# Two attention layers on one core: where the prologue's maxima are kept, and the order of a head's loads

## The chip, the cores and the metric

The kernel runs on one core of a Trainium2 chip. The metric is the device time of one execution in microseconds (us), as the median of several runs. A core has five engines that work side by side and wait for each other by semaphores: TensorE (PE, the matmuls; PEld is its weight load), VectorE (DVE), ScalarE (ACT), GpSimd (POOL) and SyncE (SP), which here only issues transfers (DMA).

## The reference

A two-layer transformer on 2048 tokens of width 128. The change touches only the attention of both layers, which has 16 heads of width 64:

```python
# layer 0
scores = jnp.einsum('bhsd,bhtd->bhst', q, k) * scale
attn = jax.nn.softmax(scores, axis=-1)
out = jnp.einsum('bhst,bhtd->bhsd', attn, v)
# layer 1: q and k are rotated, and a bias by distance is added
dist = jnp.abs(pos[None, :] - pos[:, None])
kb = -p * jnp.log1p(a * dist)
attn = jax.nn.softmax(scores + kb[None], axis=-1)
out = jnp.einsum('bhqk,bhkd->bhqd', attn, v)
```

Around it stand layer norms, a gated feed-forward part in each layer (in layer 1 eight experts with a router), and the projections.

## The kernel before, in words

The program is a row of stages, each a block that starts when all engines have finished the one before. `attention_stage` is called twice, with `bias=False` and `bias=True`; its names begin with `a0_` and `a1_`, and the profile leaves the number out.

The stage before has written q and k to the chip's memory, each split in two float16 tensors, high and low halves (`qk_high`, `qk_low`). The stage works by head (16) and, in a head, by chunks of 512 queries (4): 64 chunks `n`. A chunk has eight steps `s` of 256 keys.

**Loads.** SyncE loads a head `h` by eight transfers of 256 KB: twice `qh`, `kh`, `ql`, `kl`, for the lower and the upper 64 partitions (L595 to L598), and in layer 1 the bias table `tab` of 1984 KB as a ninth (L600). All count on one semaphore, `loaded`. There is room for two heads. Head 1 is issued when head 0 has landed, head `h` from 2 on when the scores of head `h - 2` have been read.

**Maxima.** The softmax takes each query's maximum off first. `maxima(n, j)`, `j` from 0 to 7, is a pair of matmuls of the high halves alone (L612, L613), 128 queries by 1024 keys into the PSUM buffer `jb`. VectorE reduces them to one maximum per query, in layer 0 by `reduce_max` (L774), in layer 1 by an operation that adds the bias from `tab` and takes the maximum in one (L769); that one writes its sums to `junk`, which nobody reads, and the maximum by a second small instruction, the accumulator read. There is one `jb`, so each pair waits for the reduction before it (L608). When the eight are done, `merge(n)` on VectorE (L780), `divide_maxima(n)` on ScalarE (L721), `row(n)` on TensorE (L621) and `row(n)` on ScalarE (L726) make of them the rows that are subtracted.

**Scores.** `scores(n, s)` is eight matmuls into one of two halves of `st` (L639): high by high, high by low, low by high, and the maxima. In layer 0 ScalarE exponentiates out of `st` (L740). In layer 1 VectorE adds the bias out of `st` into an SBUF ring (L794, `add_bias`), and ScalarE exponentiates there (L733). `values` multiplies by v (L650), GpSimd sums the exponentials (L847), `project` and VectorE's L798 and L804 make the output.

**Order.** It is written out by hand for each engine. Maxima run two chunks ahead of the scores (`AHEAD = 2`). So there is a prologue, in which only maxima run: chunk 0's eight, `row(0)`, chunk 1's eight. Then in the main loop each step of chunk `n` also issues `maxima(n + 2, s)`. In layer 0 the first of these stands ahead of the first scores; in layer 1 `scores(0, 0)` and `scores(0, 1)` stand ahead of it.

Of the kernel before, what the change touches and what calls it, by code (L numbers as in the profile page):

```python
# [6 lines left out]
BF16 = mybir.dt.bfloat16  # L7
ALU = mybir.AluOpType
ACT = mybir.ActivationFunctionType
AX = mybir.AxisListType  # L10

P = 128
# [3 lines left out]
DH = 64  # L16
NT = S // P
QC = 512
NC = S // QC
# [15 lines left out]
AHEAD = 2  # L35
NJ = 8
# [509 lines left out]
def attention_stage(nc, k, layer, bias=False):  # L546

    with ExitStack() as ctx:
        m = Memory(nc, ctx)
        g = f"a{layer}_"  # L550
        qh, ql = m.sb(g + "qh", [P, 2 * S], F16), m.sb(g + "ql", [P, 2 * S], F16)
        kh, kl = m.sb(g + "kh", [P, 2 * S], F16), m.sb(g + "kl", [P, 2 * S], F16)
# [8 lines left out]
        st = m.ps(g + "st", [P, 2, 2 * QC])  # L561
# [2 lines left out]
        xb = m.ps(g + "xb", [P, QC])  # L564
        if bias:
            tab = m.sb(g + "tab", [P, 2, BW])
            junk = m.sb(g + "junk", [P, 2 * QC], BF16)
        ones_set, loaded = m.sem(g + "ones_set"), m.sem(g + "loaded")
        max_ready, max_done = m.sem(g + "max_ready"), m.sem(g + "max_done")
        merged, m4_done = m.sem(g + "merged"), m.sem(g + "m4_done")  # L570
        row_ready, row_done = m.sem(g + "row_ready"), m.sem(g + "row_done")
# [2 lines left out]
        pv_done, ov_saved = m.sem(g + "pv_done"), m.sem(g + "ov_saved")  # L574
        proj_ready, proj_done, rs_done = m.sem(g + "proj_ready"), m.sem(g + "proj_done"), m.sem(g + "rs_done")
        st_read = added if bias else exp_done
        loads = 8 + (1 if bias else 0)
        pool_adds = NS - 1
        block = ctx.enter_context(nc.Block())

        def summed_by(step):
            n, s = divmod(step, NS)
# [2 lines left out]
        @block.sync  # L585
        def _(sp):
            for h in range(H):
                if h >= 1:
                    sp.wait_ge(loaded, 16 * loads * h)
                if h >= 2:  # L590
                    sp.wait_ge(st_read, NS * NC * (h - 1))
                at = slice((h % 2) * S, (h % 2 + 1) * S)
                pr, half = h // 2, slice((h % 2) * DH, (h % 2 + 1) * DH)
                for low in (slice(0, DH), slice(DH, P)):
                    sp.dma_start(qh[low, at], k.qk_high[0, pr][half, :]).then_inc(loaded, 16)  # L595
                    sp.dma_start(kh[low, at], k.qk_high[1, pr][half, :]).then_inc(loaded, 16)
                    sp.dma_start(ql[low, at], k.qk_low[0, pr][half, :]).then_inc(loaded, 16)
                    sp.dma_start(kl[low, at], k.qk_low[1, pr][half, :]).then_inc(loaded, 16)  # L598
                if bias:
                    sp.dma_start(tab[:, h % 2, :], k.bias_rows(h)).then_inc(loaded, 16)  # L600

        @block.tensor
        def _(pe):
            def maxima(n, j):
                if j == 0 and n % NC == 0:
                    pe.wait_ge(loaded, 16 * loads * (n // NC + 1))
                if NJ * n + j >= 1:
                    pe.wait_ge(max_done, NJ * n + j)  # L608
                base = (n // NC % 2) * S
                q0 = base + (n % NC) * QC + (j // 2) * P  # L610
                k0 = base + (j % 2) * 2 * QC
                nc.tensor.matmul(jb[:, 0:QC], qh[0:DH, q0:q0 + P], kh[0:DH, k0:k0 + QC], start=True, stop=True)  # L612
                nc.tensor.matmul(jb[:, QC:2 * QC], qh[DH:P, q0:q0 + P], kh[DH:P, k0 + QC:k0 + 2 * QC],  # L613
                                 start=True, stop=True).then_inc(max_ready, 1)

            def row(n):
# [8 lines left out]
            def scores(n, s):  # L625
                step = NS * n + s
                base = (n // NC % 2) * S
                q0 = base + (n % NC) * QC
                if s == 0:
                    pe.wait_ge(row_done, n + 1)  # L630
                if step >= 2:
                    pe.wait_ge(st_read, step - 1)
                for r, (keys, queries) in enumerate(((kh, qh), (kh, ql), (kl, qh), (lower, rows))):
                    for t in range(2):
                        half = slice(t * DH, (t + 1) * DH)
                        k0 = base + (2 * s + t) * P
                        w = lower[half, :] if r == 3 else keys[half, k0:k0 + P]
                        x = rows[half, n % 2, :] if r == 3 else queries[half, q0:q0 + QC]
                        last = nc.tensor.matmul(st[:, step % 2, t * QC:(t + 1) * QC], w, x,  # L639
                                                start=(r == 0), stop=(r == 3))  # L640
                last.then_inc(st_ready, 1)
# [122 lines left out]
        def _(ve):  # L764
            def maxima(n, j):
                ve.wait_ge(max_ready, NJ * n + j + 1)
                if bias:
                    c0 = 2 * QC + (n % NC) * QC + (j // 2) * P - (j % 2) * 2 * QC
                    nc.vector.tensor_tensor_reduce(  # L769
                        out=junk[:, :], in0=jb[:, :], in1=tab[:, n // NC % 2, c0:c0 + 2 * QC][:, ::-1], scale=1.0,  # L770
                        scalar=-3.0e38, op0=ALU.add, op1=ALU.max, accum_out=mx[:, j // 2, j % 2:j % 2 + 1])\
                      .then_inc(max_done, 1)
                else:
                    nc.vector.reduce_max(mx[:, j // 2, j % 2:j % 2 + 1], jb[:, :], AX.X).then_inc(max_done, 1)  # L774

            def merge(n):
                ve.wait_ge(max_done, NJ * n + NJ)
# [395 lines left out]
```

## Time and profile before

| | us |
|---|---|
| three runs, median | 3418.86 |
| their lowest and highest | 3417.58, 3419.49 |
| the profiled execution, time | 3421.26 |
| its span in the trace | 3419.4 |
| attention, layer 0: first load issued to start of the loop | 193.0 to 237.8 |
| attention, layer 1: first load issued to start of the loop | 2050.6 to 2098.7 |
| layer 1's loop ends about | 3409 |

Over the span TensorE is busy 92%, GpSimd 70%, VectorE 69%, ScalarE 42%. Times in the rows count from the start of the span. A line number is that of the kernel before. A busy TensorE is not TensorE at its peak. PEclk is the clock that it was granted, as a share of 2.4 GHz; 0.50 is 1.2 GHz.

### The profile page before, as it was taken

What the parts mean: (1) busy time and instruction counts of PE and PEld (TensorE: products, weight loads), DVE (VectorE), ACT (ScalarE), POOL (GpSimd) and SP (SyncE); (2) the same over time, 40 slices, a digit from 0 to 9 for tenths busy, and PEclk for the clock granted to TensorE, in tenths of its full rate; (3) what the DMA queues carried; (4) which work ended last, traced back from release to release, by engine and by line L of the source; (5) the groups of instructions that cost most, each with busy time, mean ns of one, the idle gap of its engine ahead of it and who ended that gap; (6) DMA issues with size and microseconds to landing.
All of it is one profiled execution on the core that took longest, in us unless ns stands there. A gap on an engine that the chain in (4) does not pass through costs nothing. (4 is left out here: it accounts for less than half of the span.)

```text
span 3419.4 us, 47107 instructions
## 1 busy us (share of the span) xinstructions
PE 3133.3 (92%) x18389; PEld 1247.1 (36%) x18389; DVE 2356.3 (69%) x3610; ACT 1427.8 (42%) x1609; POOL 2394.8 (70%) x1080
## 2 busy tenths in 40 slices
PE   5949999999999999948888985999999999999997
PEld 3414444444444444333333431333333333333333
DVE  6545555555555555351211696999999999999996
ACT  3325555555555555510000222555554555545544
POOL 0019999999999999900000383888888888888887
PEclk9969999999999999958888997999999999999998
DMA  3341111112111111010000133111111111112200
GB/s 80 126 123 26 25 26 26 26 26 49 26 26 26 26 26 25 1 51 0 0 0 0 49 148 97 49 49 49 49 49 49 49 49 49 49 54 60 60 23 13
DMA packets 53617, 148.69 MB, mean 43 GB/s; under 512 B 17155, under 2 KB 24076, under 8 KB 51220
## 3 DMA queue, kind: packets, MB, share of 16 engines
q1 hardware_dynamic: 53396, 145.67, 15.5%
q8 instruction: 147, 2.41, 0.3%
q14 instruction: 74, 0.61, 0.1%
HBM read 110.78 MB, written 34.87 MB: 43 GB/s over the span
## 5 line engine op out<-in xcount | busy, mean ns | idle before, releaser
L847 POOL TENSOR_TENSOR a_total<-a_total,room 128x1024 f32<-128x1024 f32 x768 | 1815.3, 2364 | 141.9 <-ACT room L740 37.3
L650 PE MATMUL a_ov<-room,va 128*64 128x512 f32 x4096 | 991.6, 605 | 0.0
L774 DVE TENSOR_REDUCE a_mx<-a_jb 128x1 f32<-128x1024 f32 x512 | 627.2, 1225 | 508.6 <-PE a_jb L613 508.6
L733 ACT ACTIVATE room<-room,sscale 128x1024 f32<-128x1024 f32 x512 | 588.4, 1149 | 650.5 <-DVE room L794 650.4
L740 ACT ACTIVATE room<-a_st,sscale 128x1024 f32<-128x1024 f32 x512 | 548.8, 1111 | 556.6 <-PE a_st L639 556.6
L769 DVE CUSTOM_DVE_ANT_0 a_junk<-a_jb,a_tab 128x1024 bf16<-128x1024 f32 x512 | 623.8, 1218 | 50.9 <-PE a_jb L613 34.6
L794 DVE TENSOR_TENSOR room<-a_st,a_tab 128x1024 f32<-128x1024 f32 x512 | 623.7, 1219 | 5.2 <-PE a_st L639 3.0
L612 PE MATMUL a_jb<-a_kh,a_qh 64*128 64x512 f16 x1024 | 396.6, 387 | 102.0 <-DMA a_tab<-bias_line 30.9
L847 POOL TENSOR_TENSOR a_total<-room 128x1024 f32<-128x1024 f32 x128 | 302.5, 2363 | 182.4 <-ACT room L733 135.6
L639 PE MATMUL a_st<-a_qh,a_kh 64*128 64x512 f16 x2048 | 394.9, 382 | 21.0 <-DVE room L794 21.0
L650 PEld LDWEIGHTS a_ov<-room,va 128*64 128x64 f32 x4096 | 248.4, 136 | 423.6 <-issue 363.7
L613 PE MATMUL a_jb<-a_kh,a_qh 64*128 64x512 f16 x1024 | 396.7, 387 | 0.0
L639 PE MATMUL a_st<-a_qh,a_kl 64*128 64x512 f16 x2048 | 389.5, 377 | 0.0
L639 PE MATMUL a_st<-a_ql,a_kh 64*128 64x512 f16 x2048 | 389.5, 377 | 0.0
L639 PE MATMUL a_st<-a_rows,a_lower 64*128 64x512 f16 x2048 | 389.4, 377 | 0.0
L496 POOL COPY wo<-wo 128x2048 f32<-128x2048 f32 x1 | 1.9, 1891 | 409.9 <-POOLq L986 409.9
L612 PEld LDWEIGHTS a_jb<-a_kh,a_qh 64*128 64x128 f16 x1024 | 95.9, 94 | 457.8 <-issue 153.1
L639 PEld LDWEIGHTS a_st<-a_qh,a_kh 64*128 64x128 f16 x2048 | 99.4, 94 | 317.8 <-issue 155.5
L667 PEld LDWEIGHTS a_xb<-ones,a_total 128*128 128x128 f32 x1024 | 135.0, 192 | 124.1 <-issue 124.1
L671 PE MATMUL a_xb<-wo,a_osb 128*128 128x128 f32 x1024 | 178.9, 298 | 0.0
L849 POOL TENSOR_TENSOR a_total<-a_total 128x512 f32<-128x512 f32 x128 | 163.0, 1273 | 10.0
L667 PE MATMUL a_xb<-ones,a_total 128*128 128x1 f32 x1024 | 156.6, 257 | 14.5 <-issue 12.5
(181 smaller groups left out, 2616.1 us busy)
## 6 DMA issues: line engine op xcount, KB each, us to landing
a_tab<-bias_line SPq DMA_DIRECT2D x16, 1984.0 KB, 12.1
qk_high<-q_oh SPq DMA_DIRECT2D x32, 512.0 KB, 2.6
qk_low<-q_ol SPq DMA_DIRECT2D x32, 512.0 KB, 3.6
a_qh<-qk_high SPq DMA_DIRECT2D x64, 256.0 KB, 4.9
a_kh<-qk_high SPq DMA_DIRECT2D x64, 256.0 KB, 5.7
a_ql<-qk_low SPq DMA_DIRECT2D x64, 256.0 KB, 6.3
a_kl<-qk_low SPq DMA_DIRECT2D x64, 256.0 KB, 6.7
ex_w<-in_L_ffn_W SPq DMA_DIRECT2D x1, 2048.0 KB, 10.5
```

Source lines behind the costliest of these rows:

```text
L612: nc.tensor.matmul(jb[:, 0:QC], qh[0:DH, q0:q0 + P], kh[0:DH, k0:k0 + QC], start=True, stop=True)
L613: nc.tensor.matmul(jb[:, QC:2 * QC], qh[DH:P, q0:q0 + P], kh[DH:P, k0 + QC:k0 + 2 * QC], start=True, stop=True).then_inc(max_ready, 1)
L639: last = nc.tensor.matmul(st[:, step % 2, t * QC:(t + 1) * QC], w, x, start=(r == 0), stop=(r == 3))
L650: last = nc.tensor.matmul(ov[t * DH:(t + 1) * DH, :], k.va[:, 2 * s + t, h * DH:(h + 1) * DH], prob[:, step % RING, t * QC:(t + 1) * QC], ...
L667: nc.tensor.matmul(xb[:, 2 * P + t:2 * P + t + 1], total[:, n % 2, q:q + P], k.ones[:, 0:1], start=(t == 0), stop=True, skip_group_check=True)
L671: last = nc.tensor.matmul(xb[:, t * P:(t + 1) * P], osb[:, q:q + P], k.wo[:, n // NC, :], start=False, stop=True, skip_group_check=True)
L733: nc.scalar.activation(prob[:, r, :], prob[:, r, :], ACT.Exp, scale=k.sscale[:, layer:layer + 1])\
L740: nc.scalar.activation(prob[:, r, :], st[:, step % 2, :], ACT.Exp, scale=k.sscale[:, layer:layer + 1])\
L769: nc.vector.tensor_tensor_reduce(out=junk[:, :], in0=jb[:, :], in1=tab[:, n // NC % 2, c0:c0 + 2 * QC][:, ::-1], scale=1.0, scalar=-3.0e38 ...
L774: nc.vector.reduce_max(mx[:, j // 2, j % 2:j % 2 + 1], jb[:, :], AX.X).then_inc(max_done, 1)
L794: nc.vector.tensor_tensor(p[:, :, ::-1], x[:, :, ::-1], window, ALU.add).then_inc(added, 1)
L847: nc.gpsimd.tensor_tensor(t, first, prob[:, step % RING, :], ALU.add).then_inc(summed, 1)
```

## The change

- **Buffers of the maxima.** In the prologue (the first 16 maxima, `FIRST = AHEAD * NJ`) the function `scratch` gives `st[0]`, `st[1]` and `jb` in turn; from the seventeenth on `jb` alone, as before. TensorE's wait in the prologue is for the maximum three before.
- **Scores.** The first two scores wait for all 16 maxima, since `st` was in use.
- **`junk`** has two buffers; a maximum of layer 1 also waits for the one two before it.
- **Loads.** A head's four transfers of high halves come first, then the table, then the four of low halves, which count on a semaphore of their own, `low_loaded`. For head 0 SyncE waits until the first group has landed before it issues the low halves. TensorE's first maximum of a head waits for `loaded`, its first score for `low_loaded` too.

```diff
-            junk = m.sb(g + "junk", [P, 2 * QC], BF16)
-        ones_set, loaded = m.sem(g + "ones_set"), m.sem(g + "loaded")
+            junk = m.sb(g + "junk", [P, 2, 2 * QC], BF16)
+        ones_set, loaded, low_loaded = m.sem(g + "ones_set"), m.sem(g + "loaded"), m.sem(g + "low_loaded")
...
-        loads = 8 + (1 if bias else 0)
+        loads = 4 + (1 if bias else 0)
+        FIRST = AHEAD * NJ
...
+        def scratch(n, j):
+            i = NJ * n + j
+            return jb[:, :] if i >= FIRST or i % 3 == 2 else st[:, i % 3, :]
...
                     sp.wait_ge(loaded, 16 * loads * h)
+                    sp.wait_ge(low_loaded, 16 * 4 * h)
...
-                    sp.dma_start(ql[low, at], k.qk_low[0, pr][half, :]).then_inc(loaded, 16)
-                    sp.dma_start(kl[low, at], k.qk_low[1, pr][half, :]).then_inc(loaded, 16)
                 if bias:
                     sp.dma_start(tab[:, h % 2, :], k.bias_rows(h)).then_inc(loaded, 16)
+                if h == 0:
+                    sp.wait_ge(loaded, 16 * loads)
+                for low in (slice(0, DH), slice(DH, P)):
+                    sp.dma_start(ql[low, at], k.qk_low[0, pr][half, :]).then_inc(low_loaded, 16)
+                    sp.dma_start(kl[low, at], k.qk_low[1, pr][half, :]).then_inc(low_loaded, 16)
...
-                if NJ * n + j >= 1:
+                if NJ * n + j >= FIRST:
                     pe.wait_ge(max_done, NJ * n + j)
+                elif NJ * n + j >= 3:
+                    pe.wait_ge(max_done, NJ * n + j - 2)
+                o = scratch(n, j)
...
+                if n % NC == 0 and s == 0:
+                    pe.wait_ge(low_loaded, 16 * 4 * (n // NC + 1))
                 if step >= 2:
                     pe.wait_ge(st_read, step - 1)
+                else:
+                    pe.wait_ge(max_done, FIRST)
...
                 if bias:
+                    i = NJ * n + j
+                    if i >= 2:
+                        ve.wait_ge(max_done, i - 1)
```

How the instructions stand on the engines. SyncE at the start of layer 1's attention, before:

```order
L595 DMA a1_qh<-qk_high 64x2048
L596 DMA a1_kh<-qk_high 64x2048
L597 DMA a1_ql<-qk_low 64x2048
L598 DMA a1_kl<-qk_low 64x2048
L595 DMA a1_qh<-qk_high 64x2048
L596 DMA a1_kh<-qk_high 64x2048
L597 DMA a1_ql<-qk_low 64x2048
L598 DMA a1_kl<-qk_low 64x2048
L600 DMA a1_tab<-bias_line 128x3968
L595 DMA a1_qh<-qk_high 64x2048 [waits a1_loaded]
```

and now, in the same place:

```order
L601 DMA a1_qh<-qk_high 64x2048
L602 DMA a1_kh<-qk_high 64x2048
L601 DMA a1_qh<-qk_high 64x2048
L602 DMA a1_kh<-qk_high 64x2048
L604 DMA a1_tab<-bias_line 128x3968
L608 DMA a1_ql<-qk_low 64x2048 [waits a1_loaded]
L609 DMA a1_kl<-qk_low 64x2048
L608 DMA a1_ql<-qk_low 64x2048
L609 DMA a1_kl<-qk_low 64x2048
L601 DMA a1_qh<-qk_high 64x2048 [waits a1_low_loaded,a1_loaded]
```

The table has moved from the ninth place to the fifth, and the low halves stand behind a wait. TensorE at the start of layer 0's prologue, before:

```order
L612 MATMUL a0_jb<-a0_kh,a0_qh 128x512 [waits a0_loaded,a0_ones_set]
L613 MATMUL a0_jb<-a0_kh,a0_qh 128x512
L612 MATMUL a0_jb<-a0_kh,a0_qh 128x512 [waits a0_max_done]
L613 MATMUL a0_jb<-a0_kh,a0_qh 128x512
L612 MATMUL a0_jb<-a0_kh,a0_qh 128x512 [waits a0_max_done]
```

and now:

```order
L624 MATMUL a0_st<-a0_kh,a0_qh 128x512 [waits a0_loaded,a0_ones_set]
L625 MATMUL a0_st<-a0_kh,a0_qh 128x512
L624 MATMUL a0_st<-a0_kh,a0_qh 128x512
L625 MATMUL a0_st<-a0_kh,a0_qh 128x512
L624 MATMUL a0_jb<-a0_kh,a0_qh 128x512
L625 MATMUL a0_jb<-a0_kh,a0_qh 128x512
L624 MATMUL a0_st<-a0_kh,a0_qh 128x512 [waits a0_max_done]
```

The first wait for a maximum stands at the fourth pair, not at the second. TensorE at the end of layer 1's prologue, the last pair and the first scores, before:

```order
L612 MATMUL a1_jb<-a1_kh,a1_qh 128x512 [waits a1_max_done]
L613 MATMUL a1_jb<-a1_kh,a1_qh 128x512
L639 MATMUL a1_st<-a1_qh,a1_kh 128x512 [waits a1_row_done]
L639 MATMUL a1_st<-a1_qh,a1_kh 128x512
L639 MATMUL a1_st<-a1_ql,a1_kh 128x512 x2
```

and now:

```order
L624 MATMUL a1_st<-a1_kh,a1_qh 128x512 [waits a1_max_done]
L625 MATMUL a1_st<-a1_kh,a1_qh 128x512
L655 MATMUL a1_st<-a1_qh,a1_kh 128x512 [waits a1_max_done,a1_low_loaded,a1_row_done]
L655 MATMUL a1_st<-a1_qh,a1_kh 128x512
L655 MATMUL a1_st<-a1_ql,a1_kh 128x512 x2
```

The order is the same; the first score waits for three things instead of one.

## Rows read from the trace of the kernel before

**Rows 1.** Stretches: bounds, length, busy us (instructions) of PE, PEld, DVE, ACT, POOL; PEclk, DMA, GB/s

```profile
205.30:237.40 32.10, 10.30 (x36) 2.05 (x36) 19.76 (x17) 2.12 (x3) 0.00 (x0) 0.50 0.30 66
237.40:241.70 4.30, 4.26 (x20) 1.36 (x20) 1.39 (x2) 1.31 (x2) 0.00 (x0) 0.50 0.00 0
243.10:300.00 56.90, 56.81 (x398) 21.97 (x400) 33.70 (x41) 29.57 (x34) 53.59 (x25) 1.00 0.01 1
...
2112.00:3350.00 1238.00, 1209.18 (x8030) 446.20 (x8027) 1215.58 (x1883) 627.16 (x671) 1088.68 (x488) 1.00 0.17 48
```

**Rows 2.** Timeline, loads of layer 0: start, us, engine, line, what [idle before, releaser]

```profile
194.83 0.60 SPq L598 DMA_DIRECT2D a_kl<-qk_low  x1
...
197.38 0.60 SPq L598 DMA_DIRECT2D a_kl<-qk_low  x1
...
205.31 0.58 PE L612 MATMUL a_jb<-a_kh,a_qh 64*128 64x512 f16 x1 [21.48 <-DMA a_kl<-qk_low]
```

**Rows 3.** One line, L598 (kl) of layer 0's head 0: issue to landing

```profile
DMA to landing us min/median/max: 5.5/6.6/7.8
```

**Rows 4.** Timeline, loads of layer 1

```profile
2054.89 0.60 SPq L598 DMA_DIRECT2D a_kl<-qk_low  x1
2055.53 0.58 SPq L600 DMA_DIRECT2D a_tab<-bias_line  x1
...
2067.86 0.58 PE L612 MATMUL a_jb<-a_kh,a_qh 64*128 64x512 f16 x1 [30.90 <-DMA a_tab<-bias_line]
```

**Rows 5.** One line, L598 (kl) of layer 1's head 0: issue to landing

```profile
DMA to landing us min/median/max: 5.8/7.0/8.3
```

**Rows 6.** Timeline, layer 0's prologue, VectorE and TensorE

```profile
206.03 1.23 DVE L774 TENSOR_REDUCE a_mx<-a_jb 128x1 f32<-128x1024 f32 x1 [18.17 <-PE a_jb L613]
...
207.96 1.23 DVE L774 TENSOR_REDUCE a_mx<-a_jb 128x1 f32<-128x1024 f32 x1 [0.71 <-PE a_jb L613]
...
237.44 0.60 PE L612 MATMUL a_jb<-a_kh,a_qh 64*128 64x512 f16 x1 [1.32 <-DVE a_mx L774]
```

**Rows 7.** Timeline, layer 1's prologue and its end, VectorE and TensorE

```profile
2069.78 0.08 DVE L769 DVE_READ_ACCUMULATOR2_ANT a_mx<- 128x1 f32 x1
2069.92 0.10 PEld L612 LDWEIGHTS a_jb<-a_kh,a_qh 64*128 64x128 f16 x1 [1.95 <-DVE a_mx L769]
...
2070.57 1.23 DVE L769 CUSTOM_DVE_ANT_0 a_junk<-a_jb,a_tab 128x1024 bf16<-128x1024 f32 x1 [0.71 <-PE a_jb L613]
...
2072.51 1.23 DVE L769 CUSTOM_DVE_ANT_0 a_junk<-a_jb,a_tab 128x1024 bf16<-128x1024 f32 x1 [0.71 <-PE a_jb L613]
...
2084.57 0.61 PE L613 MATMUL a_jb<-a_kh,a_qh 64*128 64x512 f16 x1
...
2085.32 1.22 DVE L769 CUSTOM_DVE_ANT_0 a_junk<-a_jb,a_tab 128x1024 bf16<-128x1024 f32 x1 [1.69 <-PE a_jb L613]
...
2098.65 0.64 PE L639 MATMUL a_st<-a_qh,a_kh 64*128 64x512 f16 x2
...
2100.05 0.08 DVE L769 DVE_READ_ACCUMULATOR2_ANT a_mx<- 128x1 f32 x1
...
2100.68 1.22 DVE L794 TENSOR_TENSOR room<-a_st,a_tab 128x1024 f32<-128x1024 f32 x1 [0.35 <-PE a_st L639]
```

**Rows 8.** Timeline, VectorE in layer 1's loop

```profile
2416.52 1.22 DVE L769 CUSTOM_DVE_ANT_0 a_junk<-a_jb,a_tab 128x1024 bf16<-128x1024 f32 x1
...
2417.66 1.22 DVE L794 TENSOR_TENSOR room<-a_st,a_tab 128x1024 f32<-128x1024 f32 x1
```

**Rows 9.** Timeline, VectorE: an operation, and reductions of which each waits for the last

```profile
72.88 1.23 DVE L287 TENSOR_SCALAR rope<-rope 128x2048 f32<-128x2048 f32 x1
74.02 1.21 DVE L335 TENSOR_REDUCE tf_hi<-va 128x1 f32<-128x1024 f32 x1
75.27 1.22 DVE L336 TENSOR_REDUCE tf_lo<-va 128x1 f32<-128x1024 f32 x1
```

**Rows 10.** One line, L788, around 2415: the semaphore instruction ahead of a bias add

```profile
L788 DVEq EVENT_SEMAPHORE  x1: 50/50/50, 2415.8 to 2415.8; - x1
```

More of the change, by code:

```diff
@@ L611, in maxima @@
                 k0 = base + (j % 2) * 2 * QC
-                nc.tensor.matmul(jb[:, 0:QC], qh[0:DH, q0:q0 + P], kh[0:DH, k0:k0 + QC], start=True, stop=True)
-                nc.tensor.matmul(jb[:, QC:2 * QC], qh[DH:P, q0:q0 + P], kh[DH:P, k0 + QC:k0 + 2 * QC],
+                nc.tensor.matmul(o[:, 0:QC], qh[0:DH, q0:q0 + P], kh[0:DH, k0:k0 + QC], start=True, stop=True)
+                nc.tensor.matmul(o[:, QC:2 * QC], qh[DH:P, q0:q0 + P], kh[DH:P, k0 + QC:k0 + 2 * QC],
                                  start=True, stop=True).then_inc(max_ready, 1)
@@ L767, in maxima @@
                 if bias:
+                    i = NJ * n + j
+                    if i >= 2:
+                        ve.wait_ge(max_done, i - 1)
                     c0 = 2 * QC + (n % NC) * QC + (j // 2) * P - (j % 2) * 2 * QC
                     nc.vector.tensor_tensor_reduce(
-                        out=junk[:, :], in0=jb[:, :], in1=tab[:, n // NC % 2, c0:c0 + 2 * QC][:, ::-1], scale=1.0,
+                        out=junk[:, i % 2, :], in0=scratch(n, j), in1=tab[:, n // NC % 2, c0:c0 + 2 * QC][:, ::-1], scale=1.0,
                         scalar=-3.0e38, op0=ALU.add, op1=ALU.max, accum_out=mx[:, j // 2, j % 2:j % 2 + 1])\
@@ L773, in maxima @@
                 else:
-                    nc.vector.reduce_max(mx[:, j // 2, j % 2:j % 2 + 1], jb[:, :], AX.X).then_inc(max_done, 1)
+                    nc.vector.reduce_max(mx[:, j // 2, j % 2:j % 2 + 1], scratch(n, j), AX.X).then_inc(max_done, 1)
             def merge(n):
```

## The prediction

> **What bounds the kernel now.** Attention runs twice, in layer 0 without a bias and in layer 1 with one. I read the stretches first, for the engine that is busy in each, then the timeline of both prologues. In the main loops TensorE is busy 56.81 of 56.90 us in layer 0, and VectorE 1215.58 of 1238.00 us in layer 1 [rows 1]. So VectorE's idle time in layer 0's loop costs nothing, and what matters there is TensorE; in layer 1 it is VectorE. Before each loop stands a stretch that neither bounds: in layer 0's prologue TensorE is busy 10.30 of 32.10 us and VectorE 19.76 [rows 1], and ahead of that both wait for the loads.
>
> The loads: in layer 0 the first matmul starts at 205.31, released by the last of eight transfers of 256 KB, issued at 197.38 [rows 2]. In layer 1 the bias table is the ninth, issued at 2055.53, and the first matmul starts at 2067.86, released by it [rows 4].
>
> The maxima: TensorE fills the single buffer `jb`, VectorE reduces it, TensorE waits for that. Layer 0's reductions start at 206.03 and 207.96: 1.93 us apart, of which 1.23 is work and 0.71 waiting for the next pair of matmuls [rows 6]. Layer 1's start at 2070.57 and 2072.51, 1.94 us apart [rows 7]. Sixteen stand in each prologue.
>
> **Part 1, the loads.** The first four transfers of head 0 are now the high halves. The last of them takes the place in SyncE's queue that the first `kl` transfer has today: issued at 194.83, landed 5.5 us later, at 200.3. The last of the eight is issued at 197.38 and lands 7.8 us later, at 205.2 [rows 2, 3]. Between the two lie four landings of 1.2 us: they come in the order of issue at a constant rate. The first matmul moves from 205.3 to 200.4, **4.9 us** off layer 0. In layer 1 the eighth lands at 2054.89 + 8.3 = 2063.2; the fourth, issued 2.55 us before it as in layer 0, at 2052.3 + 5.8 = 2058.1 [rows 4, 5]. The table has landed by 2067.8, 4.6 us behind what stands ahead of it. Put behind the fourth it lands at 2062.7, **5.1 us** earlier. Bounds for both: 4.5 and 5.5 us.
>
> The low halves are issued once the rest has landed, in layer 0 from 200.4 to some 203; by today's 5.5 to 7.8 us they are there by 211. The first score that reads them comes at about 221.6, by the sum below. Ten microseconds cover them, and as many in layer 1. Behind SyncE's new wait are queued head 0's low halves and then head 1's loads, which TensorE needs two chunks into the loop, so they are covered too. Without that cover each microsecond of lateness would be one of the path.
>
> **Part 2, the rotation.** With `st[0]`, `st[1]` and `jb` TensorE may be two pairs ahead of the reduction in progress. From the start of a pair to the start of its reduction pass 0.65 us (2069.92 to 2070.57) [rows 7], less than two reductions take, so VectorE runs back to back. At what distance, no row shows for two maxima in a row. Two kinds of rows bound it. In layer 1's loop a bias add starts 1.14 us behind a maximum, whose accumulator read lies in between, and does not wait for it [rows 8]. Two reductions of which the second waits for the first start 1.25 us apart [rows 9]. The new maxima don't wait for the one before, so I take 1.15 us and keep 1.26 as the other end. A chunk of eight maxima has seven such steps. Layer 0: 2 x 7 x (1.93 - 1.15) = **10.9 us**. Layer 1: 2 x 7 x (1.94 - 1.15) = **11.1 us**. With 1.26 it would be 9.4 and 9.5. The way from a chunk's merge over ScalarE and TensorE's row to the next maximum stays, since `row(0)` still stands between the chunks.
>
> **Part 3, what now waits.** The first two scores write into `st`, so they wait for all sixteen maxima. In layer 0 a pair for chunk 2 that needs all sixteen stands ahead of them already (237.44) [rows 6]: nothing is added. In layer 1 the scores stand ahead of it. Today they start at 2098.65, while the last maximum is still to run, and the first bias add follows at 2100.68, only 0.63 us behind the last accumulator read at 2100.05 [rows 7]. In the change that read is followed by the handover to TensorE (2069.78 to 2069.92, 0.14 us) and by the scores' own 2.03 us (2098.65 to 2100.68): 2.17 us instead of 0.63, a **loss of 1.5 us**. Queued behind the waiting scores are TensorE's next maxima and values, and VectorE and ScalarE wait for the scores, so the loss is on the path. Bounds 1.2 and 1.9.
>
> **Part 4, the second `junk` buffer.** It adds a wait for `max_done` to nearly all 512 maxima of layer 1, on the engine that bounds its loop; here a small cost would weigh. What is waited for is the maximum before the last, long done. An operation with several waits gets a semaphore instruction of its own. The bias add has one today, of 50 ns; for the add that starts at 2417.66 it stands at 2415.8, nearly two operations early, and the add still starts 1.14 us behind its forerunner [rows 8, 10]. I cost it at nothing. The cover is that VectorE's queue is read ahead. Where it is not, it costs: the first maximum of chunk 1 has such an instruction that waits for its matmuls, and starts 0.75 us behind the pair (2084.57 to 2085.32), not 0.65 [rows 7].
>
> **Sum.** Layer 0: 4.9 + 10.9 = 15.8. Layer 1: 5.1 + 11.1 - 1.5 = 14.7. Together 30.5 us. The profiled run took 3421.26 us (its span of 3419.4 and 1.9 around it); 30.5 off makes 3390.8. The median of the runs, 3418.86, is 2.4 lower, so the forecast is **3388.4 us**. The bounds of the loads and of the handover make it 3387 to 3391.
>
> **The rivals.**
> *The maxima don't overlap.* They come 1.26 us apart. For it: the reductions 1.25 us apart. Against it: each of those waits for the one before, and the first of them, which does not, starts 1.14 us behind its forerunner (72.88 to 74.02) [rows 9]. It gives back 0.11 x 28 = 3.1 us: 3391.5. The Trainium skill has a rule to this effect (VectorE: DVE Perf Modes, The DRAIN you can't avoid): the next operation does not start until the pipe is empty. By that rule the time would be this rival's; this trace disagrees for the loop's operations, which take 1.22 us and start 1.14 us apart [rows 8].
>
> *TensorE's clock rises in the prologue.* Today it is granted 0.50 (1.2 GHz) through layer 0's prologue and for 4.3 us of dense work behind it, then 1.00 [rows 1]. The change packs the same 10.3 us of matmuls into some 21 us. If that raises it, the dense stretch runs at 2.4 GHz: half of 4.3 us in layer 0, as much at the start of layer 1 less what VectorE's own pace keeps, and some tenths for shorter ways from pair to reduction. Together 4 us less: 3384.4. If it rises later than today, because the prologue starts at another moment, up to 2 us more: 3390.4. The Trainium skill (TensorE: Matmul & The Clock Gate, What's actually happening) says that the throttled clock is the default and activity releases it. By that rule this rival is open; the row shows only that a third of the time busy did not do it.
>
> *The new waits cost VectorE (this one ends slower).* Place: each maximum of layer 1's loop. Price: the 0.10 us of a semaphore instruction that is not taken early, x 512 = 51 us, on an engine busy 98% of that stretch: 3388.4 + 51 = 3439. The gain is gone from 30.5 / 512 = 0.06 us each. Against it stands the bias add, which carries the same burden for nothing.
>
> *The loads don't come earlier*, because transfers in flight share the engines evenly: the 10 us go, 3398. Against it stand the landings 1.2 us apart.
>
> **How the numbers follow.** The forecast 0.60, maxima without overlap 0.12, the clock early 0.16, the loads 0.05, the waits 0.03, and 0.04 for a change that has no effect at all. The range from 3383.0 to 3394.0 takes in the first three with the bounds of the costs and leaves out 0.12. A measurement of this kernel tells about 0.2%, 7 us, from no change, and only the last two cases lie there or above: faster 0.94, same 0.03, slower 0.03.
>
> **What would show it.** The first matmul 5.6 us behind the issue of the fourth transfer in layer 0, today 10.5. The maxima of both prologues 1.15 us apart. In layer 1 the first bias add 2.2 us behind the last accumulator read. From there to the end of the stage each loop as long as now. It would be wrong if a loop got longer, if the granted clock were 1.00 ahead of the first score, or if a low half released a matmul.

## The result, and the profile after

The kernel before took 3418.25 us (median of four runs, 3417.58 to 3419.49), the changed one 3389.22 us (four runs, 3386.0 to 3390.83). The ratio is 0.9913, with an interval from 0.9896 to 0.9931: 29.0 us less. The profiled execution of the changed kernel is the 3386.0 us one, its span is 3384.2 us.

The stretches of the changed kernel that answer to [rows 1]: bounds, length, busy us (instructions) of PE, PEld, DVE, ACT, POOL, then PEclk, DMA share, GB/s. They are layer 0's prologue, the dense work behind it, a piece of its loop, and nearly all of layer 1's loop.

```profile
197.40:218.30 20.90, 9.55 (x36) 2.01 (x36) 18.44 (x17) 2.12 (x3) 0.00 (x0) 0.50 0.67 151
218.40:222.00 3.60, 3.60 (x20) 1.32 (x20) 1.31 (x2) 1.12 (x2) 0.00 (x0) 0.58 0.00 0
228.00:284.90 56.90, 56.90 (x400) 22.43 (x396) 33.95 (x43) 28.98 (x33) 53.94 (x26) 1.00 0.00 1
2080.00:3315.00 1235.00, 1206.15 (x8007) 445.23 (x8004) 1212.81 (x1880) 625.33 (x670) 1085.57 (x487) 1.00 0.17 48
```

The prologue is 20.9 us long instead of 32.1, and VectorE is busy in 18.4 of them. The two loops look as they did: TensorE busy throughout in layer 0, VectorE 98% busy in layer 1. The loads of layer 0 in the timeline (start, us, engine, line, what), with the row for L602 (`kh`) of head 0, answer to [rows 2, 3]:

```profile
192.24 0.60 SPq L602 DMA_DIRECT2D a_kh<-qk_high  x1
197.33 0.45 SPq L608 DMA_DIRECT2D a_ql<-qk_low  x1
...
197.45 0.58 PE L624 MATMUL a_st<-a_kh,a_qh 64*128 64x512 f16 x1 [16.32 <-DMA a_kh<-qk_high]
```

```profile
DMA to landing us min/median/max: 4.1/4.6/5.1
```

The fourth transfer lands 5.1 us behind its issue and releases the first matmul. In layer 1 the table releases it, issued fifth, as [rows 4, 5] had it ninth:

```profile
2032.63 0.58 SPq L604 DMA_DIRECT2D a_tab<-bias_line  x1
2041.87 0.44 SPq L608 DMA_DIRECT2D a_ql<-qk_low  x1
...
2041.99 0.58 PE L624 MATMUL a_st<-a_kh,a_qh 64*128 64x512 f16 x1 [25.35 <-DMA a_tab<-bias_line]
```

VectorE in layer 0's prologue, and the first pair of the loop on TensorE, for [rows 6] ("x2" and 2.35 are two reductions in one row):

```profile
201.57 2.35 DVE L793 TENSOR_REDUCE a_mx<-a_st 128x1 f32<-128x1024 f32 x2
203.83 1.21 DVE L793 TENSOR_REDUCE a_mx<-a_jb 128x1 f32<-128x1024 f32 x1
204.97 2.34 DVE L793 TENSOR_REDUCE a_mx<-a_st 128x1 f32<-128x1024 f32 x2
...
218.34 0.60 PE L624 MATMUL a_jb<-a_kh,a_qh 64*128 64x512 f16 x1 [2.78 <-DVE a_mx L793]
```

Three maxima take 204.97 - 201.57 = 3.40 us: 1.13 us apart, none waits for its pair. The end of layer 1's prologue, VectorE and TensorE, for [rows 7]:

```profile
2060.74 1.22 DVE L788 CUSTOM_DVE_ANT_0 a_junk<-a_jb,a_tab 128x1024 bf16<-128x1024 f32 x1
2061.88 0.08 DVE L788 DVE_READ_ACCUMULATOR2_ANT a_mx<- 128x1 f32 x1
2061.88 1.22 DVE L788 CUSTOM_DVE_ANT_0 a_junk<-a_st,a_tab 128x1024 bf16<-128x1024 f32 x1
2063.03 0.08 DVE L788 DVE_READ_ACCUMULATOR2_ANT a_mx<- 128x1 f32 x1
...
2065.25 1.22 DVE L813 TENSOR_TENSOR room<-a_st,a_tab 128x1024 f32<-128x1024 f32 x1 [1.95 <-PE a_st L655]
```

```profile
2063.26 0.61 PE L655 MATMUL a_st<-a_qh,a_kh 64*128 64x512 f16 x2 [2.92 <-DMA a_kl<-qk_low]
```

The maxima stand 1.14 us apart. The first bias add comes 2065.25 - 2063.03 = 2.22 us behind the last accumulator read, not 0.63: the scores start 0.23 us behind that read, and then VectorE waits for them. The profile names a low half as the releaser of the first score. It is a wait for three things, and which of them ended it is settled below.

VectorE in layer 1's loop, for [rows 8], and the semaphore instruction that now stands ahead of a maximum, for [rows 10]:

```profile
2384.86 1.22 DVE L813 TENSOR_TENSOR room<-a_st,a_tab 128x1024 f32<-128x1024 f32 x1
2386.00 1.22 DVE L788 CUSTOM_DVE_ANT_0 a_junk<-a_jb,a_tab 128x1024 bf16<-128x1024 f32 x1
```

```profile
L786 DVEq EVENT_SEMAPHORE  x510: 21/21/1734, 2044.0 to 3321.5; - x170
```

There are 510 of them, of 21 ns in the median, and a maximum still starts 1.14 us behind the bias add.

Where the time went, read from the timelines of both kernels in the same way: "load" from the first load's issue to the first matmul; "chunks" from there to the second chunk's merge; "handover" in layer 0 from that merge to the first exponential, in layer 1 from the last accumulator read to the first bias add; "loop" from there to the first operation of the block behind attention; "stage" the whole. (In layer 1 "chunks" and "handover" overlap by the 0.12 us between the last read and the merge.) All in us; the experiments of the next section stand in the same table.

| | L0 load | chunks | handover | loop | stage | L1 load | chunks | handover | loop | stage | both |
|---|---|---|---|---|---|---|---|---|---|---|---|
| before | 12.29 | 32.11 | 2.38 | 1225.02 | 1271.80 | 17.30 | 32.31 | 0.63 | 1309.02 | 1359.14 | 2630.9 |
| changed | 7.01 | 20.87 | 2.38 | 1224.41 | 1254.67 | 11.77 | 21.15 | 2.22 | 1309.34 | 1344.37 | 2599.0 |
| a2 (changed, again) | 7.40 | 20.88 | 2.38 | 1224.30 | 1254.96 | 11.83 | 21.15 | 2.23 | 1309.36 | 1344.45 | 2599.4 |
| e1 loads only | 7.33 | 32.11 | 2.38 | 1224.24 | 1266.06 | 12.04 | 32.30 | 0.63 | 1309.32 | 1354.17 | 2620.2 |
| e2 rotation only | 12.47 | 20.87 | 2.38 | 1225.05 | 1260.77 | 17.04 | 21.16 | 2.22 | 1308.80 | 1349.10 | 2609.9 |
| e3 two buffers | 7.40 | 20.88 | 1.25 | 1224.66 | 1254.19 | 11.97 | 21.16 | 0.31 | 1308.95 | 1342.27 | 2596.5 |
| e4 wait in prologue | 7.21 | 20.87 | 2.38 | 1225.04 | 1255.50 | 11.95 | 21.15 | 2.23 | 1309.32 | 1344.54 | 2600.0 |
| e5 filler | 7.36 | 22.20 | 2.20 | 1224.74 | 1256.50 | 13.12 | 22.05 | 1.38 | 1308.44 | 1344.87 | 2601.4 |
| e6 two buffers, filler | 7.17 | 22.00 | 0.19 | 1224.63 | 1253.99 | 11.99 | 22.36 | 0.32 | 1308.45 | 1343.00 | 2597.0 |
| e7 wait for the last | 7.21 | 23.62 | 2.38 | 1226.22 | 1259.43 | 11.98 | 24.41 | 2.23 | 1309.30 | 1347.80 | 2607.2 |
| e8 two, light filler | 7.04 | 20.87 | 1.25 | 1225.00 | 1254.16 | 11.98 | 21.15 | 0.70 | 1309.01 | 1342.73 | 2596.9 |
| e9 two, slice of qh | 5.91 | 20.87 | 1.25 | 1224.04 | 1252.07 | 10.45 | 21.15 | 0.31 | 1309.74 | 1341.54 | 2593.6 |
| e10 e8 and e9 | 5.70 | 20.87 | 1.26 | 1224.13 | 1251.96 | 10.48 | 21.16 | 0.71 | 1309.64 | 1341.87 | 2593.8 |

Attention gives 17.1 us in layer 0 and 14.8 in layer 1, 31.9 together. The span gives 35.2. The other 3.3 us lie in blocks that the change does not touch: 2.6 ahead of layer 0's first load (it is issued at 190.44, before at 193.02; over all these traces between 190.4 and 193.5), 0.6 between the two stages (582.6 to 586.8 over all) and 0.1 at the end. So two executions of the same code differ by some 3 us there, and the stages are compared by this table rather than by the spans.

### The profile page after: what moved, and what is told of

Same layout as the page of the kernel before. It is cut to its first block and busy times, and to the rows that moved or that the text cites. A ratio compares the mean times of both kernels' runs of the same rounds, so it can differ in the third digit from the quotient of the medians.

```text
span 3384.2 us, 47620 instructions
## 1 busy us (share of the span) xinstructions
PE 3129.0 (92%) x18389; PEld 1247.0 (37%) x18389; DVE 2353.5 (70%) x3610; ACT 1427.8 (42%) x1609; POOL 2395.2 (71%) x1080
## 5 line engine op out<-in xcount | busy, mean ns | idle before, releaser
L793 DVE TENSOR_REDUCE a_mx<-a_jb 128x1 f32<-128x1024 f32 x501 | 613.4, 1224 | 480.2 <-PE a_jb L625 480.2
L788 DVE CUSTOM_DVE_ANT_0 a_junk<-a_jb,a_tab 128x1024 bf16<-128x1024 f32 x501 | 610.1, 1218 | 18.8 <-PE a_jb L625 2.5
L624 PE MATMUL a_jb<-a_kh,a_qh 64*128 64x512 f16 x1002 | 383.4, 383 | 16.4 <-DVE a_mx L793 5.7
L625 PE MATMUL a_jb<-a_kh,a_qh 64*128 64x512 f16 x1002 | 383.5, 383 | 0.0
```

The costliest lines, as they stand in the source:

```text
L624: nc.tensor.matmul(o[:, 0:QC], qh[0:DH, q0:q0 + P], kh[0:DH, k0:k0 + QC], start=True, stop=True)
L625: nc.tensor.matmul(o[:, QC:2 * QC], qh[DH:P, q0:q0 + P], kh[DH:P, k0 + QC:k0 + 2 * QC], start=True, stop=True).then_inc(max_ready, 1)
L788: nc.vector.tensor_tensor_reduce(out=junk[:, i % 2, :], in0=scratch(n, j), in1=tab[:, n // NC % 2, c0:c0 + 2 * QC][:, ::-1], scale=1.0, sc ...
L793: nc.vector.reduce_max(mx[:, j // 2, j % 2:j % 2 + 1], scratch(n, j), AX.X).then_inc(max_done, 1)
```

## The experiments

The theory was that of the prediction: loads 10 us, rotation 22 us, minus 1.5 us at layer 1's first scores. All diffs are against the changed kernel unless they say otherwise. The kernel before, run beside them, took 3422.2 us in the first group (e1 to e4), 3420.26 in the second (a2 and e5 to e7) and 3419.69 in the third (e8 to e10); ratios are to those. "..." in a diff stands for lines left out.

**One part at a time (e1, e2), and the changed kernel again (a2).** e1 keeps the new order of the loads and takes the rest back, e2 the reverse.

```diff
# e1
-            return jb[:, :] if i >= FIRST or i % 3 == 2 else st[:, i % 3, :]
+            return jb[:, :]
...
# e2
...
+                    sp.dma_start(ql[low, at], k.qk_low[0, pr][half, :]).then_inc(loaded, 16)
+                    sp.dma_start(kl[low, at], k.qk_low[1, pr][half, :]).then_inc(loaded, 16)
                 if bias:
...
```

> Only the loads are changed; the maxima use the one buffer jb again, and junk's new wait is gone. My theory: the two parts are independent. The first matmul of layer 0 starts 7.0 us behind SyncE's first issue (12.3 in the kernel before, 7.0 in the changed one), of layer 1 11.8 us behind it (17.3 and 11.8), so 5.3 and 5.5 us are gained; maxima stay 1.93 and 1.94 us apart; the first bias add again stands 0.63 us behind the last accumulator read. Both layers together 10.8 us below before. Rival, that in layer 1 the low halves and not the maxima release the first scores (the trace of the changed kernel names a kl transfer there): then with the slow maxima, where the scores come 11 us later, that name is gone, and the full kernel holds a part of the loss of 2.2 us that comes from the loads.

> Only the rotation over three buffers (with junk's second buffer and wait); the loads are those of before, all on one semaphore. My theory: first matmul 12.3 and 17.3 us behind SyncE's first issue as before; maxima 1.13 us apart in layer 0 and 1.145 in layer 1; first bias add of layer 1 some 2.2 us behind the last accumulator read, since it waits for the sixteenth maximum: 11.2 + 11.2 - 1.6 = 20.8 us below before. Rival, that the low halves cause the wait of the first scores: here all halves have landed before the first maximum, so the bias add would come at about 0.6 us behind the read, and the gain would be 22.4 us.

> The changed kernel once more, beside the next two. My theory: the stages of attention take 1254.7 and 1344.4 us as in its first trace, within 0.5; what differs from run to run lies before layer 0's attention (190.4 us in its first trace, 193.0 in that of the kernel before) and between the two. So the median is 31 to 32 us below before, where the 29 us of the first measurement were taken against few runs. Rival, that the attention stages themselves differ from run to run: then they differ by more than 1 us between two traces of one kernel.

e1: 3408.88 us, ratio 0.9961 (0.9946 to 0.9976). e2: 3399.47, 0.9934 (0.9917 to 0.995). a2: 3388.78, 0.9907 (0.9893 to 0.9922). By the table e1 gives 10.7 us, e2 21.1, together 31.8; both parts in one kernel give 31.9. They add up, neither covers the other. By the medians e1 lies 13.3 us below the kernel before and e2 22.7, which is more than the table's 10.7 and 21.1; the kernel before was slowest in that group, and the blocks outside attention vary by some 3 us. a2's stages are those of the first trace within 0.3 us, and its median is 31.5 us below the kernel before, as expected; so the 29.0 us of the first measurement lie below what both give. In e1 the maxima still come 1.93 us apart, in e2 the loads land as before.

e2 also settles who ends the wait of layer 1's first score. There every half has landed before the first maximum, and VectorE still reads:

```profile
2077.39 0.08 DVE L782 DVE_READ_ACCUMULATOR2_ANT a_mx<- 128x1 f32 x1
2077.51 0.16 DVE L793 TENSOR_REDUCE a_m<-a_mx 128x4 f32<-128x8 f32 x1
2079.61 1.23 DVE L807 TENSOR_TENSOR room<-a_st,a_tab 128x1024 f32<-128x1024 f32 x1 [1.95 <-PE a_st L649]
```

```profile
2077.62 0.61 PE L649 MATMUL a_st<-a_qh,a_kh 64*128 64x512 f16 x2 [2.91 <-DVE a_mx L782]
```

The same 2.22 us, and here the profile names the maximum (`a_mx`) as the releaser of the first score. It is the wait for the sixteenth maximum, and the low half that the profile names in the changed kernel is a wrong label: head 0's low halves are issued by 2043.6 and land within 5.3 us, fourteen microseconds ahead of 2063.26.

**Two buffers (e3).** If VectorE runs back to back with three buffers, it may with two, as a pair takes 0.65 us and a reduction 1.13. Then `st[0]` stays free, and `scores(0, 0)` need wait for no maximum.

```diff
-            return jb[:, :] if i >= FIRST or i % 3 == 2 else st[:, i % 3, :]
+            return jb[:, :] if i >= FIRST or i % 2 == 0 else st[:, 1, :]
...
-                if NJ * n + j >= FIRST:
+                if NJ * n + j > FIRST:
                     pe.wait_ge(max_done, NJ * n + j)
-                elif NJ * n + j >= 3:
-                    pe.wait_ge(max_done, NJ * n + j - 2)
+                elif NJ * n + j >= 2:
+                    pe.wait_ge(max_done, NJ * n + j - 1)
...
-                else:
+                elif step == 1:
                     pe.wait_ge(max_done, FIRST)
```

> The changed kernel with two buffers in turn instead of three, jb and st[1], so that st[0] is free and the first scores wait for no maximum; the second scores wait for all sixteen. My theory: from the end of a reduction to the next one out of the same buffer pass 0.14 us of handover and 0.65 us of matmuls, 0.79 in all, less than the 1.14 that the other buffer's reduction takes; so two buffers feed VectorE as well as three. Maxima stay 1.13 and 1.145 us apart; layer 1's first bias add comes 0.3 to 0.6 us behind the last accumulator read instead of 2.2, layer 0's loop starts 1.1 us earlier. Some 3 us below the changed kernel. Rival, that two are too few (the time until TensorE sees a finished reduction is longer when it comes from a wait at the head of its queue): maxima 1.2 us apart or more, 28 x 0.07 = 2 us or more given back, no gain over the changed kernel.

3386.05 us, ratio 0.9893 (0.9879 to 0.9908). VectorE's chunks are as short as with three buffers (20.88 and 21.16 us), and the bias add follows the last read at once:

```profile
2065.71 0.08 DVE L788 DVE_READ_ACCUMULATOR2_ANT a_mx<- 128x1 f32 x1
2065.83 0.16 DVE L799 TENSOR_REDUCE a_m<-a_mx 128x4 f32<-128x8 f32 x1
2066.02 1.22 DVE L813 TENSOR_TENSOR room<-a_st,a_tab 128x1024 f32<-128x1024 f32 x1
```

The handover in layer 1 is 0.31 us, 1.91 shorter. In layer 0 it is 1.25, 1.13 shorter: there the pair for chunk 2 goes into `jb`, which the fifteenth maximum used, so it waits for fifteen maxima and no longer for all sixteen (`> FIRST` in the diff). Together the two stages are 2.6 us shorter than in the changed kernel; that is by the table, since the intervals of the ratios overlap. The third buffer bought nothing, and its price was 3.0 us of handovers, of which the prediction had counted 1.5.

**The new waits of VectorE's maxima (e4, e7).** e4 drops the second wait in the loop, where another bias add always stands between. e7 goes the other way: each maximum of both layers waits for the one before it.

```diff
# e4
-                    if i >= 2:
+                    if 2 <= i < FIRST:
# e7, in both layers
+                i = NJ * n + j
+                if i >= 1:
+                    ve.wait_ge(max_done, i)
```

> The changed kernel with junk's added wait only on the first sixteen maxima of layer 1; in the loop none, as before. My theory: the wait is taken early and costs nothing; layer 1's loop, from its first bias add to the first operation of the next stage, is 1309.3 us as in the changed kernel (1309.0 before), within 0.3. Rival, the wait costs VectorE something in the loop: up to 0.10 us x 496 = 50 us; the trace of the changed kernel leaves room for at most 0.3 us of it, and this run would show the loop at 1309.0 or below.

> The changed kernel, but each maximum waits for the one right before it, in both layers. My theory: what lets maxima start 1.13 us apart is that none waits for its forerunner; with the wait they are 1.24 to 1.27 us apart in both prologues, as the reductions of the weights are (1.25), and the prologues are 28 x 0.12 = 3.4 us longer. In layer 1's loop a bias add stands between two maxima and the wait is over before it matters: loop 1309.3 as in the changed kernel. Rival, that VectorE's reductions from PSUM overlap whatever is waited for: 1.13 us again. Second rival, that the wait costs the loop something as well: up to 0.1 x 496 = 50 us.

e4: 3387.83 us, ratio 0.9901 (0.9886 to 0.9915); layer 1's loop is 1309.32 us with 14 such waits and 1309.34 with 510. The waits are free within what this loop varies over all these traces (1.3 us, 3 ns for each of 496 waits). e7, one run, took 3396.97 us. Its maxima in layer 0's prologue, and in layer 1's:

```profile
203.09 1.23 DVE L793 TENSOR_REDUCE a_mx<-a_jb 128x1 f32<-128x1024 f32 x1
204.42 2.55 DVE L793 TENSOR_REDUCE a_mx<-a_st 128x1 f32<-128x1024 f32 x2
207.07 1.23 DVE L793 TENSOR_REDUCE a_mx<-a_jb 128x1 f32<-128x1024 f32 x1
...
2054.64 1.23 DVE L788 CUSTOM_DVE_ANT_0 a_junk<-a_st,a_tab 128x1024 bf16<-128x1024 f32 x1
2055.79 0.08 DVE L788 DVE_READ_ACCUMULATOR2_ANT a_mx<- 128x1 f32 x1
2056.02 1.22 DVE L788 CUSTOM_DVE_ANT_0 a_junk<-a_st,a_tab 128x1024 bf16<-128x1024 f32 x1
```

1.33 and 1.38 us apart instead of 1.13 and 1.14, and not 1.24 to 1.27 as expected. In layer 1's loop the same wait costs nothing (1309.30 us), because there an add lies between two maxima. Nor is it the semaphore instruction by itself: the changed kernel has one in layer 1's prologue too, for the maximum two before, and stays at 1.14. So it is the wait for the engine's own last operation that makes 1.33 of 1.13. Layer 0's loop is 1.8 us longer in e7. Its trace shows most of the reason: TensorE's clock is still 0.50 for 8.2 us of the loop's first work (4.3 in the kernel before), so a second set of eight scores runs at it, with 0.43 us from one to the next instead of 0.21.

```profile
223.40:231.60 8.20, 6.88 (x32) 2.24 (x34) 3.77 (x4) 2.34 (x3) 2.34 (x1) 0.50 0.00 0
```

That is one trace, and why the clock rose later there is not shown.

**The clock (e5, e6, e8).** In the changed kernel as before, the granted clock is 0.50 (1.2 GHz) until after the first scores in both layers. Extra matmuls, which nobody reads, might raise it earlier. e5 adds two of 128 rows behind each prologue pair, e6 the same on two buffers, e8 one of 64 rows on two buffers.

```diff
# e5, e6
+                if NJ * n + j < FIRST:
+                    for _ in range(2):
+                        nc.tensor.matmul(ov[:, :], qh[:, q0:q0 + P], kh[:, k0:k0 + QC], start=True, stop=True)
# e8
+                if NJ * n + j < FIRST:
+                    nc.tensor.matmul(ov[:, :], qh[0:DH, q0:q0 + P], kh[0:DH, k0:k0 + QC], start=True, stop=True)
```

> The changed kernel with two further matmuls (128 x 512, into the buffer ov, which nobody reads then) behind each of the 16 pairs of maxima, so that TensorE is busy all through the prologue. My theory: the granted clock is 1.00 before the first scores in both layers; the first exponential of layer 0 comes 1.3 us behind the second merge instead of 2.4, layer 1's first bias add 1.4 us behind the last accumulator read instead of 2.2, and the first steps of the loops run at the full clock; together some 3 us below the changed kernel (my blind price was 4). The maxima stay 1.13 and 1.145 us apart, since VectorE sets them; the filler costs at most 0.3 us at each start, while the clock is low. Rival: the clock is not what the start of the loop waits for, and the run is the same as the changed kernel or slower by the filler.

> Both additions: two buffers (jb and st[1]) and the filler. The gains of two buffers (2.2 us by stages) and of the filler overlap in layer 1, where the first bias add already follows the last accumulator read by 0.31 us. My theory: 4 us below the changed kernel, 35 to 36 below before. Rival, that they add in full: 5 us; or that the filler behind the last pair now delays the first scores, which no longer wait for anything else: no more than two buffers alone.

> The two buffers of e3_two_buffers, and behind each of the sixteen prologue pairs one more matmul (64 rows, 512 columns, into the idle PSUM buffer ov, read by nobody). At clock 0.50 a step of TensorE is then about 0.86 us, less than the 1.13 us between maxima, so VectorE should keep its pace: maxima 1.13 (layer 0) and 1.145 us (layer 1) apart as in e3. Clock theory: the added work raises the granted clock to 1.00 before the first scores, so layer 1's loop (first bias add to the combine) is 0.9 us shorter than e3's 1308.95, as e5_filler and e6 showed, layer 0's (first exponential to the combine) up to 1 us shorter than 1224.66: both attention stages together about 2 us below e3's 1254.19 + 1342.27. Rival: the clock stays 0.50 until the first scores, and both stages are e3's within 0.5 us.

e5: 3391.69 us, ratio 0.9913 (0.9897 to 0.993). e6: 3386.49, 0.99 (0.9885 to 0.9915). e8: 3384.91, 0.9892 (0.9875 to 0.9908). Stretches of e5: layer 0's first five microseconds of matmuls, the next three, and the stretch in which TensorE waits for the last maximum and starts the scores.

```profile
200.00:206.00 6.00, 5.14 (x15) 0.92 (x16) 3.67 (x3) 0.00 (x0) 0.00 (x0) 0.50 0.64 160
206.00:209.00 3.00, 3.00 (x14) 0.68 (x14) 2.97 (x3) 0.00 (x0) 0.00 (x0) 0.96 0.17 34
...
222.00:226.00 4.00, 2.92 (x16) 1.25 (x18) 2.41 (x3) 0.74 (x1) 0.00 (x0) 0.66 0.00 0
```

The clock does rise in the prologue, some five microseconds in. Until then the fillers hold the pairs 1.50 us apart, and VectorE waits. Between the chunks it falls, and the same happens once more. Behind the last pair TensorE waits 1.95 us for the sixteenth maximum, the clock falls, and layer 0's first scores run slowly after all, with matmuls of 0.64 us: 1.3 us lost in the chunks, 0.2 won at the handover. In layer 1 the clock is still 1.00 when the scores start (their matmuls take 0.39 us): the chunks are 0.9 us longer, the handover is 0.84 and the loop 0.90 shorter (the loop varies by 0.9 without any filler, so that part is weak). On both layers that is 0.6 us worse (-0.84 and +1.48); the rest of e5's 2.3 us are its loads, 1.35 in layer 1 and 0.35 in layer 0. The 3 us that e5 was expected to win did not come. In e6, on two buffers, the first scores of both layers run at 1.00, and still its stages are 0.2 us shorter and 0.7 longer than e3's: what the scores win the chunks have lost, 1.1 and 1.2 us. Its rival expectation held, no more than two buffers alone. In e8 the light filler leaves VectorE its pace (20.87 us), but the clock does not rise at all before the scores:

```profile
199.00:206.60 7.60, 6.96 (x22) 0.77 (x18) 7.60 (x7) 0.00 (x0) 0.00 (x0) 0.50 0.65 143
209.00:218.10 9.10, 8.39 (x27) 1.40 (x28) 8.38 (x8) 1.88 (x2) 0.00 (x0) 0.50 0.79 167
```

TensorE is busy 92% of both stretches, at 0.50 throughout. The stages are e3's within 0.5 us: e8's rival expectation held. (Its median is 1.1 us below e3's, but the two ratios' intervals overlap almost wholly.) Why e5's matmuls raised the clock and e8's did not stays open. They differ in their rows and in their number. Rows alone do not settle it, since the scores, which do raise the clock, have 64 rows as well; but of them two overlap all the time, while e8's filler runs alone.

**A slice of qh first (e9, and e10 with e8's filler).** The maxima of chunk 0 read only 512 of 2048 columns of `qh`.

```diff
# against e3
-                    sp.dma_start(qh[low, at], k.qk_high[0, pr][half, :]).then_inc(loaded, 16)
+                    if h == 0:
+                        sp.dma_start(qh[low, 0:QC], k.qk_high[0, pr][half, 0:QC]).then_inc(loaded, 16)
+                    else:
+                        sp.dma_start(qh[low, at], k.qk_high[0, pr][half, :]).then_inc(loaded, 16)
...
                     sp.wait_ge(loaded, 16 * loads)
+                    for low in (slice(0, DH), slice(DH, P)):
+                        sp.dma_start(qh[low, QC:S], k.qk_high[0, pr][half, QC:S]).then_inc(rest_loaded, 16)
...
+                if j == 0 and n == 1:
+                    pe.wait_ge(rest_loaded, 32)
```

> The two buffers of e3_two_buffers, and head 0's first loads take only the first 512 columns of qh, two transfers of 64 KB in place of 256 KB, since the maxima of chunk 0 read no more; the other 1536 columns follow behind the first group, and TensorE waits for them ahead of chunk 1. Rate theory (landings 1.2 us apart per 256 KB, so 0.3 per 64 KB): the first matmul comes 2 x 0.9 = 1.8 us earlier in each layer, that is first issue to first matmul 5.6 us in layer 0 (7.4 in e3) and 10.2 in layer 1 (11.97), together 3.6 us below e3, and this is the fastest version. Rival: the time to landing is set by the issues (0.64 us each) and a fixed latency of some 5 us, and shorter rows are moved more slowly: less than 1 us for both layers.

> The edits of e8_two_buffers_light_filler and e9_two_buffers_q_slice together on two buffers. If both theories hold, 3.6 + 2 us below e3 by the stages; if only the loads do, 3.6; if neither, e3's stages within 0.5 us.

e9: 3382.05 us, ratio 0.9887 (0.9872 to 0.9902). e10: 3383.63, 0.9891 (0.9876 to 0.9906). The loads are 1.5 us shorter in each layer than in e3 (5.91 and 10.45 instead of 7.40 and 11.97), where 1.8 was expected: the second `kh` transfer lands 4.0 us behind its issue, not 5.1. Layer 0's first loads in e9:

```profile
192.92 0.60 SPq L606 DMA_DIRECT2D a_kh<-qk_high  x1
196.90 1.08 SPq L612 DMA_DIRECT2D a_qh<-qk_high  x2
...
197.02 0.58 PE L632 MATMUL a_jb<-a_kh,a_qh 64*128 64x512 f16 x1 [15.12 <-DMA a_kh<-qk_high]
```

Where the missing 0.3 us went is not shown; the four issues, 0.6 us each, are not shortened by smaller transfers, which may be it. By the table e9 is 2.9 us shorter than e3 and 5.4 shorter than the changed kernel; the 3.6 us expected against e3 were not reached. It is the fastest kernel here, by its median too, though the runs' intervals overlap with e3's. e10 adds nothing to it.

## Why the prediction was right

Forecast 3388.4 us, range 3383.0 to 3394.0; measured 3389.22. The sum was 30.5 us, the stages give 31.9. Step by step:

**Loads.** Forecast 4.9 and 5.1 us, measured 5.28 and 5.53: 10.8 instead of 10.0. The mechanism, landings in the order of issue at a constant rate, held: the two `kh` transfers, the second and the fourth, land 4.1 and 5.1 us behind their issues at 190.97 and 192.24, which is 1.1 us for each 256 KB. The size came from the eight-transfer queue, by which the fourth lands 5.5 us behind its issue; it landed after 5.1. Part of the difference is chance: over the nine traces with these loads the first matmul follows the first issue by 7.01 to 7.40 us in layer 0 and by 11.77 to 12.04 in layer 1, leaving out e5's 13.12, where SyncE's third issue took 1.49 us and not 0.59. Measured by them, the gain in layer 0 is 4.9 to 5.3, so its forecast lies within what a load varies. The cover of the low halves was there: they landed by 204.7, when SyncE issues the next head's first load; the first score that reads them stands at 218.7.

**Rotation.** Forecast 10.9 and 11.1 us by a spacing of 1.15, measured 11.24 and 11.16 (32.11 - 20.87 and 32.31 - 21.15). Layer 1's 1.14 us was hit; layer 0's plain reductions come 1.13 apart, and seven steps twice make 0.3 us of that. Layer 0 is the term that the bias add's row [rows 8] sized a little too small.

**The loss at layer 1's first scores.** Forecast 1.5, measured 2.22 - 0.63 = 1.59. The 0.1 us lie in the score's start, 0.23 us behind the read and not 0.14. The 0.14 was read from a pair that waits for one semaphore, the score waits for three (in e2, at the same 0.23 us, for two); that the number of waits is the reason is likely but was not tested. e3 shows that the loss could be avoided, and 1.1 us in layer 0 with it, where the prediction had put the handover down as unchanged.

**The second junk buffer.** Forecast nothing, measured nothing (e4). The cover named for it was that the waits are long satisfied when VectorE reads them. e7 is the case without that cover: there each costs 0.20 to 0.24 us in the prologue, and nothing in the loop, where it is satisfied early again.

**The rest.** Layer 0's loop gives 0.6 us, layer 1's takes 0.3 more. Over the traces with the same code in the loop these lengths differ by 1.0 us, so neither needs a cause.

**From the sum to the time.** The sum was taken from the profiled execution's own 3421.26 us, and the 2.4 us to the median then subtracted. The profiled execution of the changed kernel was its fastest instead, for reasons outside the stages. 31.9 us off 3421.26 and 2.4 off make 3387.0; the median was 2.3 us above this, within what the untouched blocks vary. So the sum was 1.4 us too small and the median 2.3 us too high, and the two cancel in part. That the forecast lies only 0.8 us from the measured time is luck; the terms were right to 0.4 us each.

**The rivals.** *No overlap*: at 1.26 us it would have been 3.1 us longer; the maxima came at 1.13 and 1.14. e7 built the case, where each waits for the last, and it costs 2.75 + 3.26 = 6.0 us in the chunks, since the spacing is then 1.33 and 1.38. Its price was set too low, by the reductions 1.25 us apart [rows 9], whose only wait is the one for the last, where e7's have two waits; that this makes the difference is not tested. The Trainium skill's sentence that the next operation does not start until the pipe is empty (VectorE: DVE Perf Modes, The DRAIN you can't avoid) is not what this kernel shows for operations that don't wait for each other; the same paragraph goes on that a next operation which is not held starts earlier, and the prediction left that half out. *The clock in the prologue*: it stayed at 0.50 until the scores in both layers, as forecast. e5, e6, e8 and e10 show that it is not to be had cheaply: in the stages of the table no kernel with a filler is faster than the same kernel without it. e7 shows the other half of that rival, a clock that rises later, at 1.8 us of layer 0's loop. *Waits on VectorE*: e4. *No earlier loads*: e1 gives 10.7 us.

**The signs.** Two of the signs of being wrong that the prediction names seem to be there. A low half stands in the profile as releaser of a matmul, and e2 shows this label to be wrong. Layer 1's loop is 0.3 us longer, less than it varies. The chance of "faster" should have been 0.93 and not 0.94, by the chances 0.03 and 0.04 of the two cases that it leaves out.

## What to carry to other kernels

Where a slow reader and a quick writer share one buffer, a second buffer took the whole gap here, where the writer's step with its handover (0.65 and 0.14 us) is shorter than the reader's (1.13); a third only took memory that somebody else then waited for. Look for what the borrowed buffer holds up behind the rotation (here the first scores), and borrow the piece that is needed last. Ahead of a stage's start, order its transfers by who reads them first, and cut off what the first chunk does not read: each 256 KB moved behind the start was worth 1.0 to 1.4 us here (1.5 for e9's 384 KB, 5.3 and 5.5 for four times 256 KB).

## What the runs showed of the hardware

- Two operations of VectorE over 128 x 1024 elements, each 1.21 to 1.23 us long in the trace, start 1.13 to 1.14 us apart if they are not made to wait for each other, and 1.33 (with an accumulator read, 1.38) apart if the second waits for the first by a semaphore in addition to its other wait.
- A second wait on an engine's instruction costs a semaphore instruction of 21 ns that disappears in the queue when it is long satisfied: layer 1's loop took 1309.34 us with 510 of them and 1309.32 with 14.
- An issue of one of these 256 KB loads on SyncE takes 0.59 to 0.60 us (0.45 to 0.48 the first of a group), but now and then 1.5 to 1.7 (1.71 at 198.46 in the changed kernel, 1.49 in e5's layer 1); where it stands ahead of the first matmul, as in e5, the load is 1.1 to 1.4 us longer.
- In the profile a wait for several semaphores can be labelled with the wrong one. It named a transfer at layer 1's first score; in e2, in which every half had landed long before, the wait was equally long.
- TensorE at 92% busy with matmuls of 64 rows, about half of the time one alone (e8), kept the granted clock at 0.50 for 7.6 and 9.1 us. Matmuls of 64 rows of which two overlap, at the start of the loops, were followed by 1.00 after 2.2 us (e9, layer 0), 4.3 us (before, layer 0) and some 5.6 us (e1, layer 1), and in e7's layer 0, with a pause in between, after 8.5 us.
